# q projected once with its sine term exchanged by transfers; v projected with k and transposed

## The reference, cut to what matters

```python
xn = _layernorm(x, axis=-1)
x = x + _L0_attn_ref(xn, ...) + _L0_ffn_ref(xn, ...)

def _L0_attn_ref(x, Wqa, Wqb, Wkva, Wkvb, Wout, bout):
    q = (x @ Wqa @ Wqb).reshape(b, s, H, D)
    kv = (x @ Wkva @ Wkvb).reshape(b, s, KVH, D, 2)
    k, v = (kv[..., 0], kv[..., 1])
    q = _rope(q)          # r1 = x1 * cos - x2 * sin, r2 = x1 * sin + x2 * cos
    k = _rope(k)          # over even and odd dimensions
    ...                   # each k and v serves g = 4 heads
    scores = jnp.einsum('bqhd,bkhd->bhqk', q, k) * scale
    scores = jnp.where(causal[None, None], -jnp.inf, scores)
    w = jax.nn.softmax(scores, axis=-1)
    out = jnp.einsum('bhqk,bkhd->bqhd', w, v).reshape(b, s, E)
    return out @ Wout + bout

def _L0_ffn_ref(x, w_gate, w_up, w_down):
    gate = fp4_linear(x, w_gate)      # both operands quantized to 4 bits in blocks of 16
    y = fp4_linear(x, w_up)
    return fp4_linear(silu(gate) * y, w_down)
```

## Time and profile before

| | us |
|---|---|
| median of 3 runs | 821.9 |
| lowest and highest | 819.39, 822.25 |
| the profiled execution | 822.47 |
| span of its instructions | 820.7 |
| PE, DVE, ACT, POOL busy | 746.0, 637.2, 553.2, 602.6 |

### The profile page before, as it was taken

The page is one execution under the profiler, slowest core; times in us unless marked ns, Lnnn a source line. Parts: engine busy times, 40 slices in busy tenths (PEclk is TensorE's granted clock), DMA queues, the critical chain, the costliest instruction groups (busy, mean ns, idle before and its releaser), DMA issues.

```text
span 820.7 us, 18663 instructions
## 1 busy us (share of the span) xinstructions
PE 746.0 (91%) x6641; PEld 468.1 (57%) x6733; DVE 637.2 (78%) x1396; ACT 553.2 (67%) x1169; POOL 602.6 (73%) x706
## 2 busy tenths in 40 slices
PE   2277899999999999999999999999999999999886
PEld 1143455665657565665756566666656565656444
DVE  4479788888788888888788888888887888787310
ACT  1213586777777777777777777777777777776771
POOL 5324597878879797878788797878788797856561
PEclk9668799999999999999999999999999999999997
DMA  4412323141314233241414232241413232230000
GB/s 115 124 48 77 78 75 80 54 107 50 86 45 112 58 93 76 58 111 45 98 36 109 53 105 64 63 106 50 111 49 84 47 97 60 81 75 9 21 15 14
DMA packets 66518, 58.24 MB, mean 71 GB/s; under 512 B 17554, under 2 KB 56434, under 8 KB 66426
## 3 DMA queue, kind: packets, MB, share of 16 engines
q1 hardware_dynamic: 66426, 57.04, 27.0%
HBM read 31.81 MB, written 18.61 MB: 61 GB/s over the span
## 4 chain that ended last, share of the span: by engine, by line
PE 73%; DVE 8%; ACT 6%; POOL 4%; SPq 3%; issue 3%; DMA 2%; another core or an unknown queue 0%; POOLq 0%; DVEq 0%; ACTq 0%
PE pv_ps L1038 18%; PE max_ps L1002 12%; PE exp_ps L1017 11%; PE misc_ps L1054 6%; PE max_ps L1003 6%; PE misc_ps L1103 5%; DVE neg_max L632 4%; PE misc_ps L1062 3%; PE misc_ps L1081 3%; ACT P L840 2%; PE misc_ps L1101 2%; PE misc_ps L1091 2%; PE misc_ps L1071 1%; POOL P L478 1%; PE misc_ps L1058 1%
## 5 line engine op out<-in xcount | busy, mean ns | idle before, releaser
L632 DVE TENSOR_REDUCE neg_max<-max_ps 128x1 f32<-128x512 f32 (+3 forms) x768 | 433.2, 593 | 105.2 <-PE max_ps L1003 103.6
L840 ACT ACTIVATE P<-exp_ps 128x512 f32<-128x512 f32 x512 | 293.5, 596 | 176.7 <-remote 95.5
L1017 PE MATMUL exp_ps<-Q,K 128*128 128x384 bf16 (+3 forms) x932 | 208.4, 292 | 7.5 <-ACT P L840 6.0
L1002 PE MATMUL max_ps<-K,Q 128*128 128x384 bf16 (+2 forms) x768 | 199.5, 278 | 17.2 <-DVE neg_max L632 7.0
L1003 PE MATMUL max_ps<-Kd,Q 128*128 128x128 bf16 x1024 | 190.6, 221 | 1.5 <-DVE neg_max L632 1.5
L478 POOL TENSOR_SCALAR_AFFINE_SELECT P<-P 128x512 f32<-128x512 f32 x256 | 161.7, 667 | 32.6 <-ACT P L843 32.6
L1038 PE MATMUL pv_ps<-P,V 128*32 128x512 f32 (+3 forms) x2048 | 164.2, 438 | 1.2 <-POOL P L478 0.8
L1002 PEld LDWEIGHTS max_ps<-K,Q 128*128 128x128 bf16 x768 | 75.2, 100 | 88.7 <-DVE neg_max L632 44.8
L1003 PEld LDWEIGHTS max_ps<-Kd,Q 128*128 128x128 bf16 x1024 | 99.4, 99 | 42.7 <-issue 22.8
L510 POOL TENSOR_TENSOR h<-gate_sb,up_half 128x352 f32<-128x352 f32 x64 | 59.6, 932 | 70.8 <-DVE gate_sb L645 70.8
L1017 PEld LDWEIGHTS exp_ps<-Q,K 128*128 128x128 bf16 x1024 | 82.4, 98 | 37.0 <-ACT P L840 14.3
(11 more groups left out here) (113 smaller groups left out, 1022.1 us busy)
## 6 DMA issues: line engine op xcount, KB each, us to landing
Q<-q_scr SPq DMA_DIRECT2D x64, 224.0 KB
q_scr<-q_split SPq DMA_DIRECT2D x16, 384.0 KB, 2.6
Kd<-K SPq DMA_DIRECT2D x64, 96.0 KB
x_in<-x SPq DMA_DIRECT2D x16, 256.0 KB, 5.3
q_scr<-q_split SPq DMA_DIRECT2D x16, 256.0 KB, 2.9
x_res<-x SPq DMA_DIRECT2D x16, 256.0 KB, 5.7
out<-y SPq DMA_DIRECT2D x32, 128.0 KB, 3.0
K<-k_scr SPq DMA_DIRECT2D x64, 48.0 KB
```

Source lines behind the costliest of these rows:

```text
L632: nc.vector.tensor_reduce(neg_max[:, pr // 4, i, heads[0]:heads[0] + len(heads), pr % 4], max_ps[r % 3][:, 0:len(heads) * n].rearrange("p ...
L840: nc.scalar.activation(P[g % 2][:, hh + r % 2, col:col + 512], ps[:, :], ACT.Exp, scale=SCALE).then_inc(exp_done, 1)
L1002: nc.tensor.matmul(ps[:, col:col + d], Qt, Kt[:, half, g, 0:d], start=True, stop=True)
L1017: last = nc.tensor.matmul(exp_ps[n % 2][:, col:col + width], K[par][:, half, pr // 2, kb * 128:(kb + 1) * 128], Q[par][:, pr, kb * 128:S], ...
```

## The change

q is computed by one job. Its result is multiplied by the cosine table, which gives `q_cos`, and by the sine table, which gives `q_sin`, both in slot 1. SP then exchanges neighbouring dimensions of the product: eight transfers of 16 partitions with 2 KB each, from `q_sin` to a new tile `q_swap` (`swap_q`). POOL makes `q_rope` from `q_cos` and `q_swap`. So that a dimension lies in 16 neighbouring partitions, the columns of `proj` are rearranged when they are copied, and the tables and the rows of `q_scr` follow that order. Job "kk" becomes "kkv": it has four more matmuls, for v, and moves from point 1 to point 2 of slot 2, behind "ot1" and ahead of the weighted sums. DVE reads k and v behind its last reduce of slot 2, and copies v to `vT`; job "v" is now one transpose of `vT`. The first `h_max` of the iteration moves from slot 1 to slot 2.

```diff
@@ -33,6 +33,7 @@
 MASK_SET = 5
 NCROW = 13
 WRITE_Q, WRITE_K = 3, NT
+SWAP_Q = D
 LOAD_K, LOAD_Q, COPY_K = 6, 2, 2
...
@@ -56,7 +57,7 @@
 MISC = [
     [[("gate0", 0, 1), ("up0", 1, 1)], [("xnT", 1, 2)], []],
     [[("q", 1, 2)], [("gate1", 0, 1), ("up1", 1, 1)], []],
-    [[("mrow1", 0, 0), ("qrot", 1, 2)], [("kk", 0, 2)], [("ot1", 1, -1)]],
+    [[("mrow1", 0, 0)], [], [("ot1", 1, -1), ("kkv", 0, 2)]],
     [[("gate2", 0, 1), ("up2", 1, 1)], [("v", 1, 2)], []],
     [[("gate3", 0, 1), ("up3", 1, 1)], [("onT", 1, -1)], []],
     [[("out0", 0, -1)], [("xqT", 1, 2)], []],
...
@@ -313,11 +318,17 @@
         def _(sp):
             sp.dma_start(x_in[:, :, :], x[0].rearrange("(c p) e -> p c e", p=128)).then_inc(x_loaded, 16)
             for dst, src in (
-                (wqaT_sb[:, :], wqaT), (wkvaT_sb[:, :], wkvaT), (wqb_sb[:, :], wqb), (wkvb_sb[:, :], wkvb),
+                (wqaT_sb[:, :], wqaT), (wkvaT_sb[:, :], wkvaT), (wqb_sb[:, :], wqb[:, 0:E]), (wkvb_sb[:, :], wkvb),
             ):
                 sp.dma_start(dst, src).then_inc(factors_in, 16)
...
+            def by_dimension(table):
+
+                return bass.AP(tensor=table.tensor, offset=table.offset, ap=[[NPAIR * S, D], [0, H], [1, S]])
+
             for dst, src in (
-                (cosq_sb[:, :], cosq), (sinq_sb[:, :], sinq), (cosk_sb[:, :], cosk), (sink_sb[:, :], sink),
+                (cosq_sb[:, :], by_dimension(cosq)), (sinq_sb[:, :], by_dimension(sinq)), (cosk_sb[:, :], cosk), (sink_sb[:, :], sink),
             ):
                 sp.dma_start(dst, src).then_inc(tables_in, 16)
...
@@ -380,8 +391,8 @@
                 i = T.par(2)
                 for half in range(2):
                     r = HALF * half
-                    src = bass.AP(tensor=q_scr[i].tensor, offset=half * D * NPAIR * S + 4 * hf * S,
-                                  ap=[[E * S, NSLOT + 1], [NPAIR * S, D], [1, NPAIR // 2 * S]])
+                    src = bass.AP(tensor=q_scr[i].tensor, offset=half * NPAIR * S + 4 * hf * S,
+                                  ap=[[E * S, NSLOT + 1], [H * S, D], [1, NPAIR // 2 * S]])
                     sp.dma_start(Q[i][r:r + (NSLOT + 1) * D, 4 * hf:4 * hf + 4, :], src).then_inc(qk_loaded[hf], 16)
...
+            def swap_q(T):
+
+                T.misc_wait(sp, misc_read, "q")
+                T.wait(sp, q_pool, 3, 1, 1)
+                for d in range(D):
+                    r, o = H * d, H * (d ^ 1)
+                    sp.dma_start(q_swap[r:r + H, :], q_sin[o:o + H, :]).then_inc(q_swapped, 16)
+
             def iteration(T):
                 if T.has(0):
                     T.wait(sp, x_bias_done, 1, 0, 0)
                     sp.dma_start(x_res[:, :, :], x[T.batch(0)].rearrange("(c p) e -> p c e", p=128)).then_inc(x_res_loaded, 16)
+                if T.has(2):
+                    swap_q(T)
+                if T.has(0):
                     place_max(T, 0, 1)
...
@@ -550,11 +572,10 @@
                         nc.gpsimd.tensor_copy(V[T.par(1)][:, :, s::2, 16 * s:16 * s + D],
                                               v_stage[:, :, :].rearrange("p c (g d) -> p c g d", g=KVH)[:, :, s::2, :]).then_inc(v_ready, 1)
                 if T.has(2):
-                    T.misc_wait(pool, misc_read, "q")
-                    T.misc_wait(pool, misc_read, "qrot")
-                    nc.gpsimd.tensor_tensor(q_rope[:, :], q_cos[:, :], q_sin[:, :], ALU.add).then_inc(q_pool, 1)
-                    T.wait(pool, k_muls, 1, 2, 1)
-                    T.misc_wait(pool, misc_read, "kk")
+                    T.wait(pool, q_muls, 1, 2, 1)
+                    T.wait(pool, q_swapped, 16 * SWAP_Q, 2, 16 * SWAP_Q)
+                    nc.gpsimd.tensor_tensor(q_rope[:, :], q_cos[:, :], q_swap[:, :], ALU.subtract).then_inc(q_pool, 1)
+                    T.wait(pool, k_muls, 2, 2, 2)
                     nc.gpsimd.tensor_tensor(k_rope[:, :], k_cos[:, :], k_sin[:, :], ALU.add).then_inc(k_pool, 1)
...
@@ -709,27 +730,29 @@
                     T.wait(dve, q_pool, 3, 1, 1)
                     T.misc_wait(dve, misc_filled, "q")
-                    nc.vector.tensor_tensor(q_cos[:, :], misc_ps[1][:, :], cosq_sb[:, :], ALU.mult).then_inc(misc_read[1], 1)
-                reduces(1, 2)
-                hidden_max(T, 0)
-                reduces(1, 3, 4)
+                    nc.vector.tensor_tensor(q_cos[:, :], misc_ps[1][:, :], cosq_sb[:, :], ALU.mult).then_inc(q_muls, 1)
+
+                    T.wait(dve, q_swapped, 16 * SWAP_Q, 1, 16 * SWAP_Q)
+                    nc.vector.tensor_tensor(q_sin[:, :], misc_ps[1][:, :], sinq_sb[:, :], ALU.mult).then_inc(misc_read[1], 1)
+                reduces(1, 2, 3, 4)
                 gated(T, 1)
                 reduces(1, 5)
                 reduces(2, 0, 1, 2)
-                if T.has(2):
-                    T.misc_wait(dve, misc_filled, "qrot")
-                    nc.vector.tensor_tensor(q_sin[:, :], misc_ps[1][:, :], sinq_sb[:, :], ALU.mult).then_inc(misc_read[1], 1)
+                hidden_max(T, 0)
                 reduces(2, 3)
                 hidden_max(T, 1)
                 reduces(2, 4)
+                reduces(2, 5)
                 if T.has(2):
                     T.wait(dve, k_pool, 3, 1, 1)
-                    T.misc_wait(dve, misc_filled, "kk")
+                    T.misc_wait(dve, misc_filled, "kkv")
                     nc.vector.tensor_tensor(k_cos[:, :], misc_ps[0][:, 0:128], cosk_sb[:, :], ALU.mult).then_inc(k_muls, 1)
-                    nc.vector.tensor_tensor(k_sin[:, :], misc_ps[0][:, 128:256], sink_sb[:, :], ALU.mult).then_inc(misc_read[0], 1)
-                reduces(2, 5)
+                    nc.vector.tensor_tensor(k_sin[:, :], misc_ps[0][:, 128:256], sink_sb[:, :], ALU.mult).then_inc(k_muls, 1)
+
+                    T.prev().misc_wait(dve, misc_filled, "v")
+                    nc.vector.tensor_copy(vT[:, :], misc_ps[0][:, 256:384]).then_inc(misc_read[0], 1)
...
             dve.wait_ge(factors_joined, 1)
-            nc.vector.tensor_copy(proj[:, :], max_ps[0][:, 0:2 * E + 3 * KVH * D]).then_inc(proj_ready, 1)
+
+            nc.vector.tensor_copy(proj[:, 0:E].rearrange("p (d h n) -> p h d n", d=D, h=2),
+                                  max_ps[0][:, 0:E].rearrange("p (h d n) -> p h d n", d=D, h=2)).then_inc(proj_ready, 1)
+            nc.vector.tensor_copy(proj[:, E:], max_ps[0][:, E:E + 3 * KVH * D]).then_inc(proj_ready, 1)
             iterate(dve, iteration, quantize_weights)
...
@@ -1056,20 +1082,18 @@
                     T.wait(pe, xn_done, NT, 2, NT)
                     for c in range(NT):
                         last = nc.tensor.transpose(ps[:, tok[c]], xn[:, c, :], ident[:, :])
-                elif job in ("q", "qrot"):
+                elif job == "q":
                     T.misc_wait(pe, misc_read, "xnT")
-                    c0 = E * int(job == "qrot")
-                    last = nc.tensor.matmul(ps[:, :], proj[:, c0:c0 + E], xnT[:, :], start=True, stop=True)
-                elif job == "kk":
-
-                    for n in range(2):
-                        w = proj[:, 2 * E + n * KVH * D:2 * E + (n + 1) * KVH * D]
+                    last = nc.tensor.matmul(ps[:, :], proj[:, 0:E], xnT[:, :], start=True, stop=True)
+                elif job == "kkv":
+
+                    for n in range(3):
+                        w = proj[:, E + n * KVH * D:E + (n + 1) * KVH * D]
                         for c in range(NT):
                             last = nc.tensor.matmul(ps[32 * c:32 * c + 32, n * 128:(n + 1) * 128], w, xnT[:, tok[c]], start=True, stop=True)
                 elif job == "v":
-                    for c in range(NT):
-                        last = nc.tensor.matmul(ps[:, 32 * c:32 * c + 32], xnT[:, tok[c]],
-                                                proj[:, 2 * E + 2 * KVH * D:], start=True, stop=True)
+                    T.misc_wait(pe, misc_read, "kkv")
+                    last = nc.tensor.transpose(ps[:, 0:128], vT[:, :], ident[:, :])
```

18 lines of the change are left out of this document (11 added, 7 removed).

## The result

The kernel after takes **829.0 us** (median, 828.73 to 830.52) where the kernel before takes 820.6 on the same chip: ratio 1.0109, 95% interval 1.0088 to 1.0130. That is 8.4 us slower. The forecast was 834.5, slower: the sign is right and the time lies in the range, but iteration -1 went the other way, slot 7 was not seen, and the end of the program ran at another clock. That the sum comes so near is in part luck.

What follows compares the result with a forecast made beforehand. PE was taken as the bound, with POOL, DVE and ACT close behind. Steady iterations 3.6, start 8.3 and iteration -1 0.7 sum to 12.6 us on the profiled 822.5: 835.1, with the median 0.6 lower 834.5; range 820 to 843.

Steps and rivals of the forecast that it cites:

- The start: Iteration -2: exchange delays q_rope on POOL, then batch 1's statistics, x_max and weight quantization; +8.3 us, nothing hides it.
- Iteration -1: Exchange lands 2.0 us late for q_rope; 0.7 taken, bounds 0 and 2.0, since iteration 0's loads follow.
- Slot 1: Job up1 waits on PE for DVE's q_sin to free bank 1; +0.48 us an iteration, bounds 0.2 and 0.6.
- Slot 2: ACT gates exp tile 4, reached 0.62 us earlier, then kkv adds 0.86; net +0.24 an iteration, bounds -0.3 and 0.4.
- Slot 3: Half of v's gain: exp tile 4 waits for ACT's exp 2; gain 0.46 us an iteration, or 0.2 if DVE is late.
- Slot 7: Not mentioned in the prediction; its steady iteration sum of +0.26 us has terms for slots 1 to 3 only.
- POOL and SP in the steady iterations: Exchange hidden by POOL's own queue with nothing to spare: landed at 466.7, q_rope starts at 466.75.
- The sign: Whole kernel: slower, with chance 0.73; within 0.5% (4.1 us) 0.17, faster 0.10.
- Rival 1: Steady iterations: PE stays the bound, removed 1.48 us gained in full, 20.7 us in all; 810 us, chance 0.10.
- rival 2: Iteration -2: late work of DVE or SP hides the exchange, leaving 3.6 + 0.7; 826 us, chance 0.10.
- rival 3: Iteration -2 costs as forecast, but steady iterations gain about 0.5 us each; 824 us, chance 0.12.
- rival 4: Steady iterations: exchange lands 3 us later, q_rope delays ACT's cast in slot 3 by about 1.4; 854 us, chance 0.06.

Runs made afterwards that it cites:

- a_stats: Kernel after, with POOL making the layer norm statistics ahead of q_rope in iteration -2 alone; 826.8 us, ratio 1.0091 to the kernel before.
- b_layout: Kernel before, with only the order of q's rows changed (proj columns, tables, q_scr and its access patterns), no exchange; 816.9 us, ratio 0.9971.
- a_up1: Kernel after, with job up1 one point later in slot 1, behind max tile 4's pair; 827.6 us, ratio 1.0082 to the kernel before.
- a_red: Kernel after, with job up1 one point later in slot 1 and the third max tile's reduce ahead of q_sin on DVE; 830.2 us, ratio 1.0120.
- a_qonly: Kernel after, with jobs kk and v as in the kernel before, so the q part alone; 829.2 us, ratio 1.0076 to the kernel before.
- b_kkv: Kernel before, with the k and v part alone: kkv behind ot1, v as one transpose, q unchanged; 824.5 us, ratio 1.0056.
- a_xbias: Kernel after, with POOL's x_bias moved behind xq; 820.7 us, ratio 1.0018 to the kernel before.

## Why the prediction was right or wrong

**The start: right.** Forecast +8.3, measured +8.86. The steps hold one by one:

```profile
25.57 0.40 SPq L461 DMA_DIRECT2D x_in<-x  x1
26.01 5.03 SPq L427 DMA_DIRECT2D q_swap<-q_sin  x8
```

```profile
32.52 1.26 POOL L577 TENSOR_TENSOR q_rope<-q_cos,q_swap 128x512 f32<-128x512 f32 x1 [12.48 <-DMA q_swap<-q_sin]
...
38.03 0.23 POOL L540 TENSOR_SCALAR var_eps<-bn_mv 128x4 f32<-128x4 f32 x1
```

Eight issues take 5.03 us (forecast 8 x 0.63), landing takes 1.9 (2.0), `q_rope` starts at 32.52 (31.95; SP began 0.5 later, as `x_in` itself was issued at 25.57 and not 25.07), the second `var_eps` at 38.03 (37 to 38). With `a_stats` the part of POOL's order is measured, not only argued; what I had left out is that ACT, too, has its casts of q ahead of layer norm.

**Iteration -1: wrong in sign.** Forecast +0.7, measured -2.04. POOL did wait for the exchange, for 2.81 us, but the first weighted sums did not come later for it. What I missed is the row order of `q_scr`. The prediction counts it as something that has to follow the exchange, with a possible cost of 1 us for the constants, and never asks how the load of Q reads the new rows. It reads them faster, and the one DMA wait of PE on the way to iteration 0, 1.93 us, is gone. `b_layout` shows it alone, with -1.74 for this stretch. The step that failed is the last of that paragraph, "since the loads of iteration 0 follow from it": it took from the change only when those loads can start, and took their own speed as given.

**Slot 1: mechanism right, size off.** 0.30 and not 0.48. The wait is there, on the weight load of up1, in each of the 12 steady iterations:

```profile
468.63 0.30 PEld L1080 LDWEIGHTS misc_ps<-wguT,xqT 128*128 128x128 f32 x2 [0.60 <-DVE q_sin L736]
```

It starts 0.05 behind the end of `q_sin`, so it did not go ahead during the wait, which was my case for a lower price. The size went wrong elsewhere. I took 0.86 from the chain for a job up that starts from a wait, and set its end against a max tile's start in the timeline. The chain shows the start of a tile behind a job 0.16 later than the timeline: the max tile at 460.60 stands at 460.76 there, and job up2 of before, at 470.37 in both views, is followed at 471.07 in one and at 471.23 in the other. In one view the price is 0.32. `a_up1` and `a_red` show more than the prediction knew, that a max tile waits for `q_sin` as well as up1.

**Slot 2: one term was mis-sized.** I had net +0.24, it is -0.04. `a_qonly` and `b_kkv` split it: the lost job qrot gives 0.40 (0.35 beside kkv), kkv at the end costs 0.31. My step put exp tile 4 at 465.77 in the old times, 0.62 earlier, with kkv's 0.86 behind it. In the kernel after the wait ahead of exp tile 4, 0.30, stands where I said; the one ahead of exp tile 3, 0.26, I had not seen:

```profile
473.47 0.39 PE L1043 MATMUL exp_ps<-Q,K 128*128 128x384 bf16 x2 [0.26 <-ACT P L866]
...
474.39 0.39 PE L1043 MATMUL exp_ps<-Q,K 128*128 128x256 bf16 x2 [0.30 <-ACT P L866]
...
475.26 0.86 PE L1093 MATMUL misc_ps<-xnT,proj 128*32 128x128 f32 x24
475.94 1.26 PE L1064 MATMUL pv_ps<-P,V 128*32 128x512 f32 x16
```

From kkv's start to the sums it is 0.68, not 0.86: the duration of a row overlaps the instruction behind it, and my sum took 0.86 as if it didn't. That is 0.18 of the miss of 0.28. The other 0.10 is exp tile 4 itself: it starts 0.72 earlier from the sums of slot 1 than before (4.42 and 5.14 us), not 0.62.

**Slot 3: right.** -0.47 against -0.46: exp tile 4 starts 3.99 us into the slot and not 4.45. Another 0.14 came in slot 4, which the forecast doesn't have; its cause wasn't looked for.

**Slot 7: not seen.** +0.57. The prediction asks for ACT's stalls in slots 2 and 3 and stops there: slots 4 to 7 are put at nothing without a reason. It should have followed the freed time to the next engine that is not faster: POOL, which from its second subtraction for q in slot 3 to the end of `x_bias` works for 19.5 us with hardly a gap. The collision itself was in the trace of before, `x_scale` at 0.25 where its minimum is 0.17.

**POOL and SP in the steady iterations: right, with less cover than I took.** The forecast had the landing at 466.7 and `q_rope` at 466.75. In 6 of the 14 iterations of the kernel after POOL does wait for the exchange, for 0.24 to 1.12 us, and yet an iteration with such a wait is as long as one without (45.89 to 45.93, all but the first). The 6.5 us that the prediction names between `q_sin` and its reader are counted to the new place of `q_sin`; in the rows of before it is 0.5.

**The sign** came from the start, 8.9 us. Rival 1 fell on the iteration, 45.92 and not near 44.2; rival 2 on `var_eps` at 38.03, rival 3 on the iteration too, rival 4 on the waits of `q_rope`, at most 1.12 us and not 3. Taken together: 8.3 + 0.7 + 3.6 was forecast, 8.86 - 2.04 + 2.43 measured, and the drain took 2.35 us less, which no part of the change explains. The start and slots 1 to 3 were right for their reasons; that slot 7's loss stood in for what slots 1, 2 and 4 did better than forecast was luck.

## What to carry to other kernels

When a pipeline repeats, time that is saved in one stage is a gain only if the loop that closes the period becomes shorter; follow the freed engines forward to the first one that is not earlier, and look at what they meet there. A short instruction whose mean is above its minimum in the profile is the cheapest place to look: here one instruction moved gave about 8 us. And a change of layout that only serves another change has to be costed at every transfer that reads it.

## What the runs showed of the hardware

- A VectorE `x_scale` of 128x32 takes 0.17 us, and 0.84 when it starts 0.8 us ahead of the end of GpSimd's 128x512 addition; it ended 0.04 behind that end in both kernels. Moved out of its way, it took 0.17 again (`a_xbias`). None of the 768 reduces of PSUM on VectorE took over 0.70 us beside GpSimd's instructions (median 0.60).
- The same 224 KB load is issued in 0.83 us when its slowest dimension is 7 and in 0.37 us when it is 56, and the loads of x, of 256 KB, land in 3.2 and 3.3 us instead of 5.3 and 5.7.
- A small transfer within SBUF (32 KB, 16 partitions) takes SP 0.63 us to issue and 1.9 us to land; at the start of the pipeline POOL stood idle until eight of them had been issued and had landed, and the first max tile of iteration -1 came 8.9 us later.
- The drain of the same 72 matmuls took 17.5 us at a granted clock of 0.71, 15.15 at 0.89 and 13.6 at 1.00 (`a_xbias`), beside a change that is worth 8.4 us in all.
